# Two-part heads, with scores and transposes by row halves of the array

## The chip, the core and the metric

The kernel runs on one core of a Trainium2 chip. The metric is the device time of one execution in microseconds (us); less is better. The five engines of the core that matter here are TensorE (matrix products and transposes, PE in the rows; its weight loads are PEld), VectorE (DVE), ScalarE (ACT), GpSimd (POOL) and the DMA queues (SP issues most of them). TensorE writes to PSUM, which has eight banks of 512 fp32 values for each of 128 partitions; VectorE and ScalarE read it from there.

## What is computed

Two layers, each followed by `layernorm(x + layer(x))`, on an input of 2 x 4096 x 256 (fp32). The first is a gated linear recurrence over blocks of 512 tokens. The second picks 511 tokens of each of the two batches with a router and runs a transformer block on them. The change lies in its attention, with 16 heads of 16 values:

```
hn = rmsnorm(x_sel, ln1)
q, k = rope(heads(hn @ wq), pos_sel), rope(heads(hn @ wk), pos_sel)
v = heads(hn @ wv)
sc = einsum('bhqd,bhkd->bhqk', q, k) / sqrt(16) + m_sel
a = softmax(sc); o = einsum('bhqk,bhkd->bhqd', a, v) ... @ wo
x2 = x1 + gelu(rmsnorm(x1, ln2) @ w1) @ w2          # x1 = x_sel + o
```

## The kernel before

One program with an order of instructions written out by hand for each engine; engines wait for each other on counting semaphores. The stages follow one another: recurrence (0 to about 173 us), router and choice of tokens, projections and mask for both batches (to 255), attention and FFN of batch 0 (to 366), attention and FFN of batch 1, final normalisation and scatter.

**Precision of the scores.** Products of q and k are made from parts of the numbers. Before, each q and each k is split into three bf16 parts (`parts` on VectorE, nine instructions for a chunk of 128 tokens), laid out in `SLOTS = 6` slots so that one bf16 product over 6 x 16 = 96 rows sums the six wanted products of parts. `turn_split` on TensorE transposes these for each head (32 bf16 transposes a chunk, L970), `copy_turned` brings them from PSUM to `qkT` (q on ScalarE, L1361, k on VectorE, L1805).

**The attention loop.** It runs for each batch over 4 turns `hg` of 4 heads, and in each over 16 units u: 4 chunks c of 128 queries by 4 heads h (`units`). For one unit:

1. `scores` (TensorE, L1006): one product, 128 queries by 512 keys, into one of four banks (`S_BANKS`, a ring of `RING = 4`), six units ahead (`AHEAD`).
2. `masked` (VectorE, L1857): adds the mask, writes SBUF `sm` (a ring of 8) and the row's extreme `nmax`.
3. `below`: subtracts `nmax` in place; even units on VectorE (L1865), odd ones on GpSimd (L672).
4. `turn_scores` (TensorE, L1023): four 128 x 128 fp32 transposes into bank 2 + u % 2; it waits for `below_ready`, and for the exponential of unit u - 2, which used that bank.
5. `exponentials` (ScalarE, L1377): reads the bank, writes `prT` in SBUF.
6. `values` (TensorE, L1045): for the four heads of a chunk together, 16 x 4 products of 32 columns each in four column groups, five units late (`LAG`); banks 4 and 5.

Around it stand `copy_heads`, `copy_pair` (ScalarE), `normalise_heads` (VectorE), `turn_heads` and `turn_pair` (TensorE, L1054 and L1061), once or twice a turn. In the second attention GpSimd also splits `w2` (L628, L631) between its subtractions. All eight banks are in use: 6, 7, 0, 1 for scores, 2 and 3 for turned differences, 4 and 5 for values. While batch 0 is in its FFN, `turn_split` of batch 1 is placed between the second FFN products (L1152).

## Time and profile before

| | |
|---|---|
| median of 3 runs | 479.98 us (479.44 to 481.64) |
| the profiled execution | 479.28 us |
| its span, first to last instruction | 477.5 us |
| mean granted clock of TensorE | 0.993 |
| first attention, first score product to last exponential | 255.1 to 322.4 us |
| second attention | 366.7 to 436.8 us |

The span is what the trace shows of the profiled execution; the 1.8 us between it and that execution's time lie before and behind it. Records of TensorE's products overlap, since it is pipelined: how fast they follow one another is read from their starts. In the rows by stretch the numbers are: the stretch and its length in us, the busy time of PE, PEld, DVE, ACT and POOL with the count of instructions behind each, the granted clock as a share of full speed, the busy share of the DMA engines and GB/s. In the rows by line, `out<-in` are the tiles written and read, with partitions x elements behind them, and `[t <-engine ...]` at the end of a row of a timeline is how long the engine sat idle before it and what released it.

### The profile page before, as it was taken

What the parts mean: (1) busy time and instruction counts of PE and PEld (TensorE: products, weight loads), DVE (VectorE), ACT (ScalarE), POOL (GpSimd) and SP (SyncE); (2) the same over time, 40 slices, a digit from 0 to 9 for tenths busy, and PEclk for the clock granted to TensorE, in tenths of its full rate; (3) what the DMA queues carried; (4) which work ended last, traced back from release to release, by engine and by line L of the source; (5) the groups of instructions that cost most, each with busy time, mean ns of one, the idle gap of its engine ahead of it and who ended that gap; (6) DMA issues with size and microseconds to landing.
All of it is one profiled execution on the core that took longest, in us unless ns stands there. A gap on an engine that the chain in (4) does not pass through costs nothing.

```text
span 477.5 us, 9894 instructions
## 1 busy us (share of the span) xinstructions
PE 438.4 (92%) x3557; PEld 335.4 (70%) x3557; DVE 383.8 (80%) x1173; ACT 241.3 (51%) x431; POOL 294.2 (62%) x295
## 2 busy tenths in 40 slices
PE   8798999999999987999998999997998999998893
PEld 5587888777777743476775777775796777676692
DVE  4878898788998799868989999865966999881773
ACT  3436555565545527024665665655434666564640
POOL 8366667776677742076665998842000999991374
PEclk9999999999999999998999999999999999999998
DMA  7713442234421211046981000000000000000011
GB/s 237 264 45 91 123 140 91 88 92 136 126 89 46 71 62 45 1 129 213 321 263 47 1 3 2 1 3 0 2 1 0 1 4 1 1 2 2 1 40 50
DMA packets 29256, 33.88 MB, mean 71 GB/s; under 512 B 5748, under 2 KB 24856, under 8 KB 29208
## 3 DMA queue, kind: packets, MB, share of 16 engines
q1 hardware_dynamic: 22976, 24.78, 16.0%
q0 software_dynamic: 3520, 8.40, 6.0%
q8 instruction: 29, 0.48, 0.4%
q10 hardware_dynamic: 2712, 0.06, 0.3%
q14 instruction: 19, 0.16, 0.1%
HBM read 19.59 MB, written 13.63 MB: 70 GB/s over the span
## 4 chain that ended last, share of the span: by engine, by line
PE 38%; POOL 16%; DVE 10%; issue 4%; ACT 3%; POOLq 0%; DVEq 0%
POOL arena L672 9%; PE ps L1023 7%; PE ps L1045 4%; PE ps L1006 4%; PE ps L1117 3%; PE ps L1152 3%; PE ps L708 3%; PE ps L970 2%; PE ps L842 2%; POOL arena L519 2%; PE ps L938 2%; PE ps L1123 1%; PE ps L977 1%; POOL w_lo L631 1%; PE ps L1143 1%
## 5 line engine op out<-in xcount | busy, mean ns | idle before, releaser
L672 POOL TENSOR_SCALAR arena<-arena,nmax 128x511 f32<-128x511 f32 x64 | 108.4, 1705 | 46.6 <-DVE nmax L1857 46.3
L1377 ACT ACTIVATE big<-ps 128x512 f32<-128x512 f32 x128 | 76.0, 600 | 57.5 <-PE ps L1023 54.4
L1857 DVE CUSTOM_DVE_ANT_0 arena<-ps,nmask 128x511 f32<-128x511 f32 x128 | 83.6, 681 | 7.8 <-PE ps L1006 5.5
L1023 PE MATMUL ps<-ident,arena 128*128 128x128 f32 x512 | 77.7, 274 | 2.4 <-POOL arena L672 1.6
L1023 PEld LDWEIGHTS ps<-ident,arena 128*128 128x128 f32 x512 | 59.5, 140 | 20.3 <-issue 10.1
L741 PE MATMUL ps<-wgd_hi,x_hi 128*128 128x512 f32 x128 | 51.6, 403 | 0.0
L1006 PE MATMUL ps<-arena 96*128 96x512 bf16 x128 | 48.2, 383 | 3.3 <-DVE nmax L1857 2.1
L743 PE MATMUL ps<-wgd_hi,x_lo 128*128 128x512 f32 x128 | 50.5, 395 | 0.0
L742 PE MATMUL ps<-wgd_lo,x_hi 128*128 128x512 f32 x128 | 50.4, 394 | 0.0
L519 POOL TENSOR_TENSOR arena<-arena 128x512 f32<-128x512 f32 x30 | 38.7, 1291 | 9.6 <-DVE arena L1501 7.9
L533 POOL TENSOR_TENSOR rq<-vq,minus_half 128x4 f32<-128x4 f32 x16 | 16.2, 1010 | 35.3 <-DVE v L1530 35.3
L1262 ACT ACTIVATE ob_sb<-arena,nb,rq 128x256 f32<-128x256 f32 x64 | 33.1, 590 | 8.2 <-POOL nb L537 8.1
L1865 DVE TENSOR_SCALAR arena<-arena,nmax 128x511 f32<-128x511 f32 x64 | 36.8, 575 | 0.0
L528 POOL TENSOR_TENSOR r<-v,minus_half 128x8 f32<-128x8 f32 x16 | 26.7, 1670 | 7.7 <-DVE v L1530 7.7
L1476 DVE TENSOR_TENSOR x_lo<-ps,x_hi 128x512 fp32r<-128x512 f32 x32 | 21.9, 685 | 10.6 <-ACT x_hi L1233 10.6
L708 PE MATMUL ps<-ones_b 128*128 128x512 bf16 x106 | 27.0, 379 | 2.7 <-DVE arena L1496 1.5
L1254 ACT CAST h_parts<-arena 48x512 fp32r<-48x512 f32 x16 | 9.9, 621 | 37.4 <-DVE arena L1489 37.4
L1496 DVE TENSOR_TENSOR arena<-ps,arena 128x512 f32<-128x512 f32 x32 | 21.8, 682 | 8.0 <-PE ps L760 8.0
L743 PEld LDWEIGHTS ps<-wgd_hi,x_lo 128*128 128x128 f32 x128 | 24.0, 188 | 5.7
L741 PEld LDWEIGHTS ps<-wgd_hi,x_hi 128*128 128x128 f32 x128 | 24.1, 188 | 5.0
L742 PEld LDWEIGHTS ps<-wgd_lo,x_hi 128*128 128x128 f32 x128 | 24.1, 188 | 5.0
L1245 ACT ACTIVATE arena<-ps 128x512 f32<-128x512 f32 x32 | 19.1, 598 | 16.3 <-PE ps L753 14.3
(266 smaller groups left out, 1013.0 us busy)
## 6 DMA issues: line engine op xcount, KB each, us to landing
arena<-in_L_attn_x SPq DMA_DIRECT2D x16, 512.0 KB, 4.8
out<-ob_sb SPq DMA_DIRECT2D x16, 512.0 KB, 3.1
w_sb<-in_L_ffn_w SPq DMA_DIRECT2D x2, 1024.0 KB, 10.7
mt_scratch<-nmask SPq DMA_DIRECT2D x8, 256.0 KB, 6.3
mt_scratch<-big SPq DMA_DIRECT2D x8, 256.0 KB
big<-in_L_attn_Wg SPq DMA_DIRECT2D x1, 256.0 KB, 4.2
big<-in_L_attn_WD SPq DMA_DIRECT2D x1, 256.0 KB, 5.1
wqk<-in_L_ffn_wq SPq DMA_DIRECT2D x1, 256.0 KB, 8.3
```

Of the source, the lines that this page charges most:

```text
L519: pool.tensor_tensor(s, s, u_sb[q][:, :, :], ALU.subtract).then_inc(s_ready, 1)
L672: pool.tensor_scalar(sm[n % SM_RING][:, 0:K - 1], sm[n % SM_RING][:, 0:K - 1], nmax[:, c, h:h + 1], None, ALU.subtract).then_inc(below_rea ...
L708: pe.matmul(ps[:, bank, :], ones_b[:, :], ones_wide, start=True, stop=True)
L741: pe.matmul(o, hi, wgd_hi[:, c, :], start=(c == 0), stop=False)
L742: pe.matmul(o, hi, wgd_lo[:, c, :], start=False, stop=False)
L743: pe.matmul(o, lo, wgd_hi[:, c, :], start=False, stop=False)
L1006: pe.matmul(ps[:, bank, :], qkT[0][:, hg * HG + h:hg * HG + h + 1, c * P:(c + 1) * P], qkT[1][:, hg * HG + h:hg * HG + h + 1, :], start=Tr ...
L1023: mm = pe.transpose(ps[:, 2 + u % 2, k * P:(k + 1) * P], sm[n % SM_RING][:, k * P:(k + 1) * P], ident[:, :])
L1262: last = act.activation(ob_sb[G % 2][:, t, :], s_sb[G % 2][:, t, :], ACT.Identity, bias=nb[G % 2][:, t:t + 1], scale=rq[:, b, n.start + t: ...
L1377: act.activation(prT[c % 2][:, h, :, :], ps[:, 2 + u % 2, :].rearrange("p (k n) -> p k n", k=C), ACT.Exp, scale=-1.0).then_inc(prT_ready, 1)
L1857: dve.tensor_tensor_reduce(sm[n % SM_RING][:, 0:K - 1], ps[:, S_BANKS[b][u % RING], 0:K - 1], nmask[b][:, c, 0:K - 1], 1.0, 3.4e38, ALU.ad ...
L1865: dve.tensor_scalar(sm[n % SM_RING][:, 0:K - 1], sm[n % SM_RING][:, 0:K - 1], nmax[:, c, h:h + 1], None, ALU.subtract).then_inc(below_read ...
```

## The change

- A head's q and k are split into two parts, a high one in fp32r and the fp32 rest, in `SLOTS = 4` slots of 16: 64 rows a head, so two heads (2 x 64 rows) share one 128-row transpose. `high` (ScalarE) copies the high parts into two slots, `parts` (VectorE, two subtractions) the rests. `turn_split` makes 16 fp32 transposes a chunk instead of 32 bf16 ones; `qT` and `kT` are fp32r.
- `scores` takes units in pairs: two products over 64 rows each, one in the upper, one in the lower half of the array's rows.
- `turn_scores` takes units in pairs too. The differences of a unit are transposed in halves of 64 rows by 64 x 64 pieces of the identity. `turn_halves` with r = 0 turns the upper half of the first unit (into bank 2) and the lower half of the second (into bank 3) by turns, with r = 1 the other halves. Between the two stand the score products of the pair six units ahead and a wait for `halves_turned`, that is for the first halves to be done.
- `below` is dealt out by `BELOW = "DPADPDPA"`: of eight units three to VectorE, three to GpSimd, two to ScalarE (an activation with scale -1 and `nmax` as bias, three units ahead of the exponential).

```diff
@@ -44,8 +44,7 @@
 SPLIT = 2
 POS = 11
 ABOVE = 14
-SLOTS = 6
-ER = SLOTS * HD
+SLOTS = 4
 HG = 4
 HP = 32
 TURNS = H // HG
@@ -58,6 +57,8 @@
 S_BANKS = ((6, 7, 0, 1), (0, 1, 6, 7))
 M_BANKS = (4, 6, 5, 7)
 LAG = 5
+BELOW = "DPADPDPA"
+A_AHEAD = 3
 PARTS = ((range(C),), ((C - 1,), (0, 1), (2,)))
 ORDER = tuple(tuple(c for part in parts for c in part) for parts in PARTS)
 FB = F // P
...
@@ -394,6 +396,15 @@
         def unit_number(b, hg, u):
             return (hg + b * TURNS) * UNITS + u

+        def below_count(n, who):
+
+            return n // len(BELOW) * BELOW.count(who) + BELOW[:n % len(BELOW) + 1].count(who)
+
+        def below_done(n):
+
+            who = BELOW[n % len(BELOW)]
+            return below_ready["DPA".index(who)], below_count(n, who)
+
         def second_out(b, c):

             return ps[:, S_BANKS[b][c], 0:D] if b == B - 1 else ps[:, 6 + c // 2, (c % 2) * D:(c % 2 + 1) * D]
...
@@ -677,11 +688,12 @@
                 for hg in range(2):
                     values_of(b, hg)
                 for hg in range(TURNS):
-                    for u in range(1, UNITS, 2):
-                        below(b, hg, u)
+                    for u in range(UNITS):
+                        if BELOW[u % len(BELOW)] == "P":
+                            below(b, hg, u)
                         if u == 9 and 0 < hg < TURNS - 1:
                             values_of(b, hg + 1)
-                        if b == B - 1 and hg in (1, 2):
+                        if b == B - 1 and u % 2 and hg in (1, 2):
                             split_w2((hg - 1) * FB + u // 2)
                 for half in range(2):
                     rsqrt(b, half)
...
@@ -957,18 +969,16 @@
                     project_qk(b, c, ps[:, 4 + c % 2, :])
                     project_values(b, c)

-            psb = ps[:, :, :].bitcast(BF16)
-
             def turn_split(b, c):

                 done = c + b * C
-                pe.wait_ge(e_ready, done + 1)
                 for m in ((1, 0) if done == C - 1 else range(2)):
+                    pe.wait_ge(e_ready, 2 * done + (2 if done == C - 1 else 1 + m))
                     for half in range(2):
                         pe.wait_ge((qT_ready, kT_ready)[m], done * 2)
-                        for h in range(8):
-                            mm = pe.transpose(psb[0:ER, 2 * m + half, h * P:(h + 1) * P],
-                                              e_sb[c % 2][:, m, 8 * half + h, :, :], ident_b[:, :])
+                        for g in range(4):
+                            mm = pe.transpose(ps[:, 2 * m + half, g * P:(g + 1) * P],
+                                              e_rows[c % 2][:, m, 4 * half + g, :], ident[:, :])
                         mm.then_inc(eT_done[2 * m + half], 1)

             def project_out(b, c, groups):
...
@@ -986,43 +996,62 @@
                 pe.wait_ge(kT_ready, (b + 1) * C * 2 - 1)

                 def scores(hg, u):
-                    c, h = units[u]
+
+                    for v in (u, u + 1):
+                        c, h = units[v]
+                        n = unit_number(b, hg, v)
+                        bank = S_BANKS[b][v % RING]
+                        if hg_is(hg, 0):
+                            if v < RING and bank < 2:
+                                pe.wait_ge(qT_ready, (b + 1) * C * 2 - 1 + bank)
+                            elif h == 0:
+                                pe.wait_ge(qT_ready, (b * C + c) * 2 + 1)
+                        if not first(b, hg) or v >= RING:
+
+                            pe.wait_ge(sm_ready, n - RING + 1)
+                        if hg_is(hg, 0) and bank >= 6:
+
+                            if b > 0:
+                                pe.wait_ge(x2_ready, (b - 1) * C + C)
+                            else:
+                                pe.wait_ge(nm_ready[0], C)
+                    for v in (u, u + 1):
+                        c, h = units[v]
+                        g, rows = (hg * HG + h) // 2, slice(h % 2 * 64, h % 2 * 64 + 64)
+                        pe.matmul(ps[:, S_BANKS[b][v % RING], :], qT[rows, g, c * P:(c + 1) * P], kT[rows, g, :],
+                                  start=True, stop=True).then_inc(s_done, 1)
+
+                def turn_scores(hg, u):
+
+                    for v in (u, u + 1):
+                        n = unit_number(b, hg, v)
+                        pe.wait_ge(*below_done(n))
+                        if hg_is(hg, 0) and v == 0:
+                            pe.wait_ge(qT_ready, (b + 1) * C * 2)
+                            pe.wait_ge(kT_ready, (b + 1) * C * 2)
+                        if first(b, hg) and v == 0:
+
+                            pe.wait_ge(zeroed, 3)
+                        if not first(b, hg) or v >= 2:
+
+                            pe.wait_ge(prT_ready, n - 1)
+
+                    turn_halves(b, hg, u, 0)
+
+                def turn_halves(b, hg, u, r):
                     n = unit_number(b, hg, u)
-                    bank = S_BANKS[b][u % RING]
-                    if hg_is(hg, 0):
-                        if u < RING and bank < 2:
-                            pe.wait_ge(qT_ready, (b + 1) * C * 2 - 1 + bank)
-                        elif h == 0:
-                            pe.wait_ge(qT_ready, (b * C + c) * 2 + 1)
-                    if not first(b, hg) or u >= RING:
-
-                        pe.wait_ge(sm_ready, n - RING + 1)
-                    if hg_is(hg, 0) and bank >= 6:
-
-                        if b > 0:
-                            pe.wait_ge(x2_ready, (b - 1) * C + C)
-                        else:
-                            pe.wait_ge(nm_ready[0], C)
-                    pe.matmul(ps[:, bank, :], qkT[0][:, hg * HG + h:hg * HG + h + 1, c * P:(c + 1) * P],
-                              qkT[1][:, hg * HG + h:hg * HG + h + 1, :], start=True, stop=True).then_inc(s_done, 1)
-
-                def turn_scores(hg, u):
-
-                    n = unit_number(b, hg, u)
-                    pe.wait_ge(below_ready[u % 2], n // 2 + 1)
-                    if hg_is(hg, 0) and u == 0:
-                        pe.wait_ge(qT_ready, (b + 1) * C * 2)
-                        pe.wait_ge(kT_ready, (b + 1) * C * 2)
-                    if first(b, hg) and u == 0:
-
-                        pe.wait_ge(zeroed, 3)
-                    if not first(b, hg) or u >= 2:
-
-                        pe.wait_ge(prT_ready, n - 1)
+                    if r:
+                        pe.wait_ge(halves_turned, n // 2 + 1)
                     for k in range(C):
-                        mm = pe.transpose(ps[:, 2 + u % 2, k * P:(k + 1) * P],
-                                          sm[n % SM_RING][:, k * P:(k + 1) * P], ident[:, :])
-                    mm.then_inc(belowT_done, 1)
+                        for v in range(2):
+                            at = (r + v) % 2 * 64
+                            mm = pe.transpose(ps[:, 2 + v, k * P + at:k * P + at + 64],
+                                              sm[(n + v) % SM_RING][at:at + 64, k * P:(k + 1) * P],
+                                              ident[at:at + 64, at:at + 64])
+                            if r and k == C - 1:
+                                mm.then_inc(belowT_done, 1)
+                    if r == 0:
+                        mm.then_inc(halves_turned, 1)

                 def values(hg, c):
                     turn = hg + b * TURNS
...
@@ -1079,14 +1108,16 @@

                 def turn_body(hg):
                     if hg_is(hg, 0):
-                        for u in range(AHEAD):
+                        for u in range(0, AHEAD, 2):
                             scores(hg, u)
                     for u in range(UNITS):
-                        if u + AHEAD < UNITS:
-                            scores(hg, u + AHEAD)
-                        elif not hg_is(hg, TURNS - 1):
-                            scores(hg + 1, u + AHEAD - UNITS)
-                        turn_scores(hg, u)
+                        if u % 2 == 0:
+                            turn_scores(hg, u)
+                            if u + AHEAD < UNITS:
+                                scores(hg, u + AHEAD)
+                            elif not hg_is(hg, TURNS - 1):
+                                scores(hg + 1, u + AHEAD - UNITS)
+                            turn_halves(b, hg, u, 1)
                         late(hg, u)
                         if not hg_is(hg, 0):
                             late(hg - 1, u + UNITS)
...
@@ -1358,13 +1389,24 @@
             def copy_turned(b, c):
                 for half in range(2):
                     act.wait_ge(eT_done[half], c + b * C + 1)
-                    act.copy(qkT[0][:, 8 * half:8 * half + 8, c * P:(c + 1) * P],
-                             ps[:, :, :].bitcast(BF16)[0:ER, half, :].rearrange("r (h n) -> r h n", h=8)
-                             ).then_inc(qT_ready, 1)
+                    act.copy(qT[:, 4 * half:4 * half + 4, c * P:(c + 1) * P],
+                             ps[:, half, :].rearrange("r (g n) -> r g n", g=4)).then_inc(qT_ready, 1)
+
+            def high(b, c):
+                done = c + b * C
+                act.wait_ge(rope_ready[b], c + 1)
+                for m, s in enumerate((slice(0, 4, 2), slice(0, 4, 3))):
+                    if done >= 2:
+                        act.wait_ge(eT_done[2 * m], done - 1)
+                        act.wait_ge(eT_done[2 * m + 1], done - 1)
+                    src = qk[b][:, c:c + 1, m * D:(m + 1) * D].rearrange("p o (h k) -> p h o k", h=H)
+                    act.copy(e_sb[c % 2][:, m, :, s, :].bitcast(F32R), src.broadcast_to((P, H, 2, HD))).then_inc(e_parts, 1)

             def split(b):
                 for c in range(C):
                     copy_turned(b, c)
+                    if c < 2:
...
@@ -1375,7 +1417,14 @@

                         act.wait_ge(pv_done, (hg + b * TURNS) * C + c - 1)
                     act.activation(prT[c % 2][:, h, :, :], ps[:, 2 + u % 2, :].rearrange("p (k n) -> p k n", k=C),
-                                   ACT.Exp, scale=-1.0).then_inc(prT_ready, 1)
+                                   ACT.Exp, scale=1.0 if BELOW[u % len(BELOW)] == "A" else -1.0).then_inc(prT_ready, 1)
+
+                def below(hg, u):
+                    c, h = units[u]
+                    n = unit_number(b, hg, u)
+                    act.wait_ge(sm_ready, n + 1)
+                    act.activation(sm[n % SM_RING][:, 0:K - 1], sm[n % SM_RING][:, 0:K - 1], ACT.Identity,
+                                   bias=nmax[:, c, h:h + 1], scale=-1.0).then_inc(below_ready[2], 1)

                 def copy_heads(hg, cs):
                     act.wait_ge(pv_done, (hg + b * TURNS) * C + cs[-1] + 1)
@@ -1392,7 +1441,13 @@

                 def turn_body(hg):
                     for u in range(UNITS):
+                        if BELOW[u % len(BELOW)] == "A" and u < A_AHEAD and hg_is(hg, 0):
+                            below(hg, u)
+                    for u in range(UNITS):
                         exponentials(hg, u)
+                        v = u + A_AHEAD
+                        if BELOW[v % len(BELOW)] == "A" and (v < UNITS or hg < TURNS - 1):
+                            below(hg + v // UNITS, v % UNITS)
                         if u == 2 and not hg_is(hg, 0):
                             copy_heads(hg - 1, range(C))
                         if u == 8 and hg == 2:
...
@@ -1415,6 +1470,8 @@
                     if b == B - 1:
                         act.wait_ge(gelu_ready, b * FB + f + 1)
                         act.copy(hid_hi[:, f, :], hidden_sb[:, f, :]).then_inc(hid_hi_ready, 1)
+                    elif f in (3, 5):
+                        high(b + 1, f // 2 - 1)

             for c in range(2):
                 copy_first_hnT(0, c)
...
@@ -1802,33 +1863,17 @@
             def copy_turned(b, c):
                 for half in range(2):
                     dve.wait_ge(eT_done[2 + half], c + b * C + 1)
-                    dve.tensor_copy(qkT[1][:, 8 * half:8 * half + 8, c * P:(c + 1) * P],
-                                    ps[:, :, :].bitcast(BF16)[0:ER, 2 + half, :].rearrange(
-                                        "r (h n) -> r h n", h=8)).then_inc(kT_ready, 1)
+                    dve.tensor_copy(kT[:, 4 * half:4 * half + 4, c * P:(c + 1) * P],
+                                    ps[:, 2 + half, :].rearrange("r (g n) -> r g n", g=4)).then_inc(kT_ready, 1)

             def parts(b, c):
                 done = c + b * C
                 dve.wait_ge(rope_ready[b], c + 1)
...
+                for m, (hi, lo) in enumerate(((slice(0, 4, 2), slice(1, 4, 2)), (slice(0, 4, 3), slice(1, 3)))):
+                    dve.wait_ge(e_parts, 2 * done + m + 1)
+                    src = qk[b][:, c:c + 1, m * D:(m + 1) * D].rearrange("p o (h k) -> p h o k", h=H)
+                    dve.tensor_tensor(e_sb[c % 2][:, m, :, lo, :], src.broadcast_to((P, H, 2, HD)),
+                                      e_sb[c % 2][:, m, :, hi, :], ALU.subtract).then_inc(e_ready, 1)
...
@@ -1879,7 +1924,7 @@
                 def turn_body(hg):
                     for u in range(UNITS):
                         masked(hg, u)
-                        if u % 2:
+                        if u and BELOW[(u - 1) % len(BELOW)] == "D":
                             below(hg, u - 1)
                         if u == 10 and not hg_is(hg, 0):
                             normalise_heads(hg - 1, range(C))
```

## Rows read from the trace of the kernel before

**Rows 1.** The page: busy time, share of the span and instructions of each engine.

```profile
PE 438.4 (92%) x3557; PEld 335.4 (70%) x3557; DVE 383.8 (80%) x1173; ACT 241.3 (51%) x431; POOL 294.2 (62%) x295
```

**Rows 2.** Busy us of each engine in stretches of the span, and granted clock.

```profile
263.00:318.00 55.00, 54.66 (x741) 42.09 (x738) 49.62 (x148) 34.68 (x61) 50.04 (x31) 1.00 0.01 2
...
376.00:420.00 44.00, 42.40 (x548) 31.69 (x546) 41.50 (x118) 26.72 (x46) 44.00 (x40) 1.00 0.01 2
...
215.00:219.00 4.00, 4.00 (x13) 2.20 (x12) 2.91 (x11) 0.00 (x0) 1.85 (x2) 0.57 0.79 292
```

**Rows 3.** The chain that ended last, in the first attention: start us, us, what.

```profile
262.94 1.01 PE ps L1045 x32
...
266.77 1.01 PE ps L1045 x32
```

**Rows 4.** Timeline of the first attention, TensorE and ScalarE: start us, us, engine, line.

```profile
273.63 0.38 PE L1006 MATMUL ps<-arena 96*128 96x512 bf16 x1
...
273.85 0.60 PE L1023 MATMUL ps<-ident,arena 128*128 128x128 f32 x4
...
274.38 0.81 PEld L1045 LDWEIGHTS ps<-big,arena 128*32 128x32 f32 x32 [0.17 <-issue]
274.38 1.08 PE L1045 MATMUL ps<-big,arena 128*32 128x128 f32 x32
...
277.22 1.10 ACT L1377 ACTIVATE big<-ps 128x512 f32<-128x512 f32 x2
```

**Rows 5.** Groups of instructions by line and form: busy us, mean ns, idle before.

```profile
L672 POOL TENSOR_SCALAR arena<-arena,nmax 128x511 f32<-128x511 f32 x64 | 108.4, 1705 | 46.6 <-DVE nmax L1857 46.3
...
L1023 PE MATMUL ps<-ident,arena 128*128 128x128 f32 x512 | 77.7, 274 | 2.4 <-POOL arena L672 1.6 <-ACT big L1377 0.7
...
L1865 DVE TENSOR_SCALAR arena<-arena,nmax 128x511 f32<-128x511 f32 x64 | 36.8, 575 | 0.0
```

**Rows 6.** Timeline near the end of the first attention: handoffs between TensorE and ScalarE.

```profile
316.13 0.60 ACT L1377 ACTIVATE big<-ps 128x512 f32<-128x512 f32 x1 [1.00 <-PE ps L1023]
...
316.84 0.42 PEld L1023 LDWEIGHTS ps<-ident,arena 128*128 128x128 f32 x4 [0.55 <-issue]
316.87 0.63 PE L1023 MATMUL ps<-ident,arena 128*128 128x128 f32 x4 [0.34 <-ACT big L1377]
316.88 1.26 ACT L1377 ACTIVATE big<-ps 128x512 f32<-128x512 f32 x2
```

**Rows 7.** Timeline of the first microseconds, TensorE: four transposes of 16 rows.

```profile
6.11 0.60 PE L781 MATMUL ps<-ident,nmask 16*128 16x16 f32 x4
```

**Rows 8.** ScalarE: a row of its timeline, one of the groups by line.

```profile
104.29 2.07 ACT L1262 ACTIVATE ob_sb<-arena,nb,rq 128x256 f32<-128x256 f32 x4
...
L1417 ACT CAST hid_hi<-big 128x512 fp32r<-128x512 f32 x8 | 5.0, 621 | 0.3
```

**Rows 9.** Timeline: first scores and last exponential of both attentions, one GpSimd start.

```profile
255.11 1.03 PE L1006 MATMUL ps<-arena 96*128 96x512 bf16 x4
...
321.79 0.60 ACT L1377 ACTIVATE big<-ps 128x512 f32<-128x512 f32 x1 [0.49 <-PE ps L1023]
...
366.68 0.60 PE L1006 MATMUL ps<-arena 96*128 96x512 bf16 x2
...
368.95 10.31 POOL L672 TENSOR_SCALAR arena<-arena,nmax 128x511 f32<-128x511 f32 x6 [37.68 <-DVE nmax L1857]
...
436.15 0.60 ACT L1377 ACTIVATE big<-ps 128x512 f32<-128x512 f32 x1 [0.49 <-PE ps L1023]
```

**Rows 10.** Timeline of the split: last chunk of batch 0, then of batch 1.

```profile
251.54 1.96 PE L970 MATMUL ps<-ident_b,arena 128*96 128x128 bf16 x32 [0.43 <-DVE arena L1805]
...
359.31 1.92 ACT L1361 COPY arena<-ps 96x1024 bf16<-96x1024 bf16 x2 [3.38 <-PE ps L970]
...
361.37 1.96 PE L970 MATMUL ps<-ident_b,arena 128*96 128x128 bf16 x32 [0.76 <-ACT arena L1361]
```

**Rows 11.** Timeline of TensorE just before its slow stretch.

```profile
211.94 3.90 PE L842 MATMUL ps<-arena 128*128 128x60 bf16 x32
```

More of the change, by code:

```diff
@@ L145, in build @@
         hid_hi, hid_lo = under(("hid_hi", [P, FB, K], F32R), ("hid_lo", [P, FB, K], F32R))
+        qT, kT = under(*[(n, [P, H // 2, K], F32R) for n in ("qT", "kT")])
         arena = sb("arena", [P, (XBUF + 4) * T * D])
@@ L248, in build @@
         rope_a, rope_b = (arena2[:, n * 1024:(n + 1) * 1024].rearrange("p (c n) -> p c n", c=2) for n in range(2))
[L249 to L250 removed]
+        e_rows = [arena2[:, 4096 + e * 2048:6144 + e * 2048].rearrange("p (m g r) -> p m g r", m=2, g=H // 2)
+                  for e in range(2)]
+        e_sb = [arena2[:, 4096 + e * 2048:6144 + e * 2048].rearrange(
             "p (m h s k) -> p m h s k", m=2, h=H, s=SLOTS) for e in range(2)]
[L252 to L253 removed]
         at_hi = arena2[:, 0:B * P * NT // 2].bitcast(BF16).rearrange("p (b h n) -> p b h n", b=B, h=P)
@@ L324, in build @@
         sm_ready = sem("sm_ready")
-        below_ready = sems("below_ready")
+        below_ready = sems("below_ready", 3)
         belowT_done = sem("belowT_done")
+        halves_turned = sem("halves_turned")
         prT_ready = sem("prT_ready")
@@ L1367, in split @@
                     copy_turned(b, c)
+                    if c < 2:
+                        high(b, c + 2)
             def attention(b):
@@ L1427, in _ @@
                 value(0, c - 1)
+            high(0, 0)
             copy_qk(0, C - 1)
             value(0, C - 1)
+            high(0, 1)
             copy_mask_rows(0, range(3))
@@ L1443, in _ @@
             copy_turned(0, 0)
+            high(0, 2)
             copy_qk(1, 2)
@@ L1446, in _ @@
             copy_turned(0, 1)
+            high(0, 3)
             value(1, 3)
@@ L1946, in _ @@
                     angles(1)
+                elif c == 2:
                     parts(0, 0)
```

35 lines of the change are left out of this document (6 added, 29 removed).

## The prediction, made before the changed kernel was run

> **What bounds the kernel now.** I read the page first: TensorE is busy 92% of the span [rows 1]. Such a share mixes stages, so the next view is the busy time by stage [rows 2]. In the steady part of the first attention (263 to 318 us) TensorE works 54.66 of 55 us; in that of the second (376 to 420 us) GpSimd works all 44. ScalarE has time left in both (34.68 of 55 us, 26.72 of 44).
>
> The chain of waits says the same of the first attention: it runs through TensorE, one group of values (L1045) every 3.83 us, so 0.96 us a unit [rows 3]. The timeline shows what fills that: score product, transposes and a quarter of the values take 0.22, some 0.46 and 0.27 us (products from 273.63 on, transposes from 273.85, 1.08 for the values of four units) [rows 4]. In the second attention it is 32 subtractions of 1.7 us on GpSimd [rows 5], with the weight split between them.
>
> What the reader should look at for this change is the pair of PSUM banks between the transposes (TensorE) and the exponentials (ScalarE). Before, unit u uses bank 2 + u % 2: while ScalarE reads one bank, TensorE fills the other. That is why a unit can cost 0.96 us although its transposes take 0.63 from first start to last end and its exponential another 0.60 behind them [rows 6].
>
> **The change: a ring.** A pair of units now writes half of each unit's transposes into both banks, waits, and then writes the other halves. `turn_scores` therefore waits, ahead of the first half, for both exponentials of the pair before (for the pair's second unit, `prT_ready` at n - 1 is the exponential of unit u - 1). And the exponentials of either unit wait for `belowT_done`, which only the last step of the second half raises. Transposes of a pair, its two exponentials, transposes of the next pair: these no longer overlap. Queued behind the waiting transposes stand the next scores, six units ahead, so nobody waits for them. The price is the length of this ring, from the end of one pair's last exponential to that of the next:
>
> - End of an exponential to the first weight load: 0.11 us (316.13 + 0.60 to 316.84); 0.03 more to the first transpose [rows 6].
> - First half: 8 transposes of 64 rows, four steps of two row halves. Fewer rows do not shorten a transpose: four with 16 rows and a 16-wide identity took 0.60 us [rows 7], four of 128 by 128 take 0.60 to 0.63 [rows 4, 6]; less the 0.27 us of the last one [rows 5] either follow one another at 0.11 us. So a step costs 0.11 us if the two halves of the array load and multiply at the same time, and 0.22 if one weight load follows the other. No row of this trace shows two row halves. The nearest, four column groups in L1045, do multiply side by side (32 in 1.08 us) but load weights one after the other (32 in 0.81 us) [rows 4]. Those share the array's rows, these do not, so I take 0.11 and keep 0.22 as a rival. Three steps of 0.11 and 0.27 for the last: 0.60.
> - The wait for `halves_turned`: a handoff of 0.11 like the one above, and 0.03. The two score products stand in it. The last step of the first half starts 0.47 us into the ring and the second half could start at 0.88; a score product needs 0.22 of TensorE [rows 4], so two side by side cost nothing. If they run one after the other, the second half starts at 0.47 + 0.11 + 0.44 = 1.02, 0.14 late: the upper bound.
> - Second half: 0.60. Handoff to ScalarE: 0.04 (316.87 + 0.63, and the second exponential's start, 316.88 + 1.26 - 0.60) [rows 6].
> - Two exponentials back to back: 1.10 (277.22) [rows 4].
>
> Sum: 0.11 + 0.03 + 0.60 + 0.14 + 0.60 + 0.04 + 1.10 = 2.62 us for two units, where two cost 1.92. The values (1.08 for two pairs) run while ScalarE holds the banks and cost nothing.
>
> The Trainium skill (TensorEngine Tiling, Key Properties) says that different tiles can load weights and multiply in parallel; no row here shows it for row halves. By that sentence the ring is 2.62 us, by serial loads 3.50. The same page of the Trainium skill (Restrictions and Gotchas, Gotcha 1) speaks against the change: row tiles cannot use one PSUM bank at once, so row tiling takes more banks; all eight are taken here.
>
> **Onto the ring come** things that ScalarE does between a pair's two exponentials. `BELOW` hands ScalarE two subtractions in eight units. That of unit 7 is issued behind exponential 4, inside a pair: 8 in an attention. The trace has no such operation; near it are 0.62 us for 512 elements in SBUF and 2.07 us for four activations of 256 elements with two column operands [rows 8]. I take 0.65, bounds 0.5 and 0.8: 5.2 us an attention. The other one stands between pairs, under the transposes. The copies of heads and pairs behind units 2, 8 and 10 are inside pairs as well: four of 512 elements at 0.50 (1.10 - 0.60, as for a second exponential) and a shorter one, 2.2 us.
>
> **An attention** is then 32 x 2.62 + 5.2 + 2.2 = 91.2 us behind its start. The first pair needs a subtraction of GpSimd, as odd units do now. In the second attention that starts at 368.95, 2.27 us behind the first scores; with 1.72 for it and 0.11, the ring starts after 4.1 us [rows 5, 9], and I take the same for the first. That makes 95.3 us each. Now they take 67.3 (255.11 to 321.79 + 0.60) and 70.1 (366.68 to 436.15 + 0.60) [rows 9]. Loss: 28.0 + 25.2 = 53.2 us. What follows the last exponential is unchanged.
>
> Taking subtractions off VectorE and GpSimd (64 each before, 48 each after, 32 on ScalarE) gains nothing, since in 2.62 us a pair neither is late: GpSimd's three in eight units are 5.2 of 10.5 us, even with the weight split, and VectorE's work was 49.62 us for some 57 units [rows 2], 1.74 a pair.
>
> **The split of heads.** VectorE's nine instructions a chunk become two, with two copies of `high` on ScalarE. ScalarE's two copies of turned heads, 1.92 us together [rows 10], become two of 512 elements, 1.10 like the exponentials [rows 4]. TensorE's 32 bf16 transposes took 1.96 us [rows 10]; 16 in fp32 take 15 x 0.11 + 0.27 = 1.92: nothing. Between the attentions the second FFN product covers all this but for the last chunk, which waits for ScalarE's copies (359.31 to 361.23, transposes at 361.37): 0.8 us gained. Ahead of the first attention TensorE waited 0.43 us for VectorE's copy before the last chunk [rows 10]: 0.4 gained at most there. `high` stands on ScalarE ahead of projections, mask rows and gelus, 1.24 us for a chunk [rows 8]; ScalarE's idle time covers it; without that cover, one chunk's worth ahead of each attention is 2.5 us. I take -1.2, bounds -4 and +2.5.
>
> **Sum.** The profiled execution took 479.28 us (its span 477.5, 1.8 around it), 0.7 below the median 479.98. 479.28 + 53.2 - 1.2 = 531.3; I say 531. Its own bounds: a handoff of 0.04 at `halves_turned` (-0.07 for 64 pairs, -4.5), the subtraction at 0.5 (-2.4), the split (-2.8); up: serial scores (+9), the subtraction at 0.8 (+2.4), the split (+3.7). 521 to 546.
>
> **The rivals.**
> - *The weight loads of the row halves follow each other.* Eight steps cost 0.11 more: 0.88 us a pair, 64 pairs, 56 us: 587. For it: the loads of L1045 [rows 4]. Against: those share the array's rows.
> - *TensorE's clock falls.* Its mean was 0.57 at 215 to 219 us, so mostly the lower of its two levels (1.2 of 2.4 GHz), behind 3.9 us in which TensorE had run 60-column products without a gap [rows 2, 11]. In the new ring it would be idle or in 64-column transposes most of the time. At half clock the eight steps cost 0.88 more a pair and the values, 2.16 us, no longer fit under 1.10, 0.5 more: 64 x 1.4 = 90 us, 621; clock falling now and then, anything from 535 on. Against: 1.00 throughout both attentions [rows 2].
> - *Faster.* Were the ring shorter than the other engines' pace, VectorE would bind: 49.62 less an eighth of 57 units at 0.575 us is 45.5 us for 57 units [rows 2, 5], 0.80 each; 64 of them instead of 0.96 are 10 us less in the first attention, 13 in the second, 455 us. It decides where the ring falls under 1.9 - 0.2 us a pair, so if sixteen transposes and their wait took 0.4 us instead of 1.3. Rows 7 speak against it, and the exponentials alone are 1.10.
>
> The Trainium skill (TensorE: Matmul & The Clock Gate, Part 4: PE-mode transpose) says that transposes do not count as busy for the clock in the same way; here the clock stays at 1.00 with transposes filling half of TensorE's time [rows 2]. By that rule the second rival is likelier than I make it.
>
> **How the numbers follow.** Ring of 2.6 us: 0.57, the forecast. Serial loads 0.25. Clock 0.11. Faster 0.05. No difference 0.02. A measurement of this kernel tells about 0.5% (2.4 us) from no change, and the first three cases are far beyond it: slower 0.93, same 0.02, faster 0.05. The first two hold 0.82 and give the range, 519 to 592; the likeliest alone has 521 to 546.
>
> **What would show it.** Right: in both attentions ScalarE idles about 1.5 us before the first exponential of each pair, waiting for the second half of the transposes; the first half waits for the second exponential; pairs follow at 2.6 us, each half takes 0.6; TensorE is busy two thirds of the time. Serial loads: halves of 1.0 us, pairs at 3.5. Clock: granted row below 1.00 in the attentions. Wrong altogether: an exponential of one pair beside transposes of the next, or pairs under 1.9 us apart.

## Result and profile after

The changed kernel takes 526.25 us (median of four runs, 524.99 to 527.43) against 479.78 us (479.44 to 481.64): 1.0959 times as long, 95% interval 1.0919 to 1.1. The profiled execution took 526.98 us, 47.7 more than that of before.

Where do the 47.7 us lie? In the timeline, an attention runs from its first score product to the end of its last exponentials (in the changed kernel L1021 and L1419, transposes L1048, values L1074):

```profile
254.63 0.73 PE L1021 MATMUL ps<-kT,qT 64*128 64x512 f32 x4
...
346.80 1.08 ACT L1419 ACTIVATE big<-ps 128x512 f32<-128x512 f32 x2 [2.90 <-PE ps L1048]
...
391.38 0.50 PE L1021 MATMUL ps<-kT,qT 64*128 64x512 f32 x2
...
483.35 1.08 ACT L1419 ACTIVATE big<-ps 128x512 f32<-128x512 f32 x2 [2.89 <-PE ps L1048]
```

That is 93.25 and 93.05 us, where before had 67.28 and 70.07 [rows 9]: 25.97 + 22.98 = 48.95 lost. The rest of the kernel gained the other 1.25: 0.48 ahead of the first attention, 0.79 between the two (391.38 - 347.88 against 366.68 - 322.39).

The timeline of three pairs of units in the first attention, TensorE at full clock (an engine's wait stands in brackets):

```profile
280.10 0.43 PE L1048 MATMUL ps<-ident,arena 64*128 64x64 f32 x7
...
280.35 0.47 PE L1021 MATMUL ps<-kT,qT 64*128 64x512 f32 x1
...
280.39 0.48 PE L1021 MATMUL ps<-kT,qT 64*128 64x512 f32 x1
...
282.35 0.36 PEld L1048 LDWEIGHTS ps<-ident,arena 64*128 64x128 f32 x8 [1.38 <-DVE arena L1910]
282.38 0.47 PE L1048 MATMUL ps<-ident,arena 64*128 64x64 f32 x8 [1.27 <-ACT big L1419]
...
282.94 0.45 PE L1048 MATMUL ps<-ident,arena 64*128 64x64 f32 x8
...
283.42 1.09 ACT L1419 ACTIVATE big<-ps 128x512 f32<-128x512 f32 x2 [0.57 <-PE ps L1048]
...
284.65 0.46 PE L1048 MATMUL ps<-ident,arena 64*128 64x64 f32 x8 [0.25 <-ACT big L1419]
```

The ring is there: first half at 282.38, second half at 282.94, both exponentials from 283.42 to 284.51, next first half at 284.65. No exponential of one pair runs beside transposes of the next. A turn takes 2.27 us. Eight half transposes take 0.47 from the first start to the last end, with their eight loads (0.36) beside them, and the two score products start 0.04 apart (280.35, 280.39).

The waits by engine say how often (total us, times, longest):

```profile
ACT big L1419 <- PE ps L1048: 85.3, 64, 2.9
DVE arena L1902 <- PE ps L1021: 57.4, 56, 2.2
PE ps L1048 <- ACT big L1419: 50.3, 48, 1.8
```

All 64 pairs make ScalarE wait for the transposes. ScalarE had waited for TensorE before the change as well (1.00 and 0.49 in [rows 6, 9]); what is new is the other direction: before, the transposes waited 0.7 us in all for ScalarE [rows 5], now 50.3. Now the same steps 15 us earlier, and the busy time by stretches (PE, PEld, DVE, ACT, POOL, then the granted clock):

```profile
267.29 0.69 PE L1048 MATMUL ps<-ident,arena 64*128 64x64 f32 x8
...
270.21 0.69 PE L1048 MATMUL ps<-ident,arena 64*128 64x64 f32 x8 [1.27 <-ACT big L1419]
...
271.79 1.93 PE L1074 MATMUL ps<-big,arena 128*32 128x128 f32 x32
273.66 0.59 PE L1048 MATMUL ps<-ident,arena 64*128 64x64 f32 x6
```

```profile
258.00:348.00 90.00, 64.04 (x1082) 50.46 (x1086) 53.27 (x155) 46.55 (x86) 41.24 (x26) 0.81 0.01 2
392.00:485.00 93.00, 65.11 (x1102) 50.99 (x1106) 54.24 (x161) 48.36 (x87) 50.83 (x42) 0.83 0.01 2
254.60:259.40 4.80, 2.08 (x25) 1.27 (x24) 4.14 (x13) 1.86 (x4) 2.27 (x2) 1.00 0.00 0
265.00:275.00 10.00, 8.72 (x126) 7.00 (x123) 4.71 (x14) 4.48 (x8) 3.85 (x3) 0.50 0.01 2
285.00:305.00 20.00, 12.81 (x282) 10.23 (x278) 13.52 (x40) 11.61 (x21) 10.98 (x8) 1.00 0.01 2
```

From 265 to 275 the granted clock is 0.50, the lower level, 1.2 GHz; before, it was 1.00 in the steady part of both attentions [rows 2]. The fall comes behind the first 4.8 us of the attention, in which TensorE was busy for 2.08 us. A turn of the ring is then 2.92 us, or 3.45 where the values (1.93 us) stand in it. So two theories have to be told apart: the ring, and the clock.

### The profile page after: what moved, and what is told of

Its sections match the earlier page's. It is cut to its first block, busy times and chain, and to the rows that moved or that the text cites. A ratio compares the mean times of both kernels' runs of the same rounds, so it can differ in the third digit from the quotient of the medians.

```text
span 525.2 us, 10691 instructions
## 1 busy us (share of the span) xinstructions
PE 436.9 (83%) x3941; PEld 337.9 (64%) x3941; DVE 360.7 (69%) x1101; ACT 256.8 (49%) x479; POOL 268.7 (51%) x279
## 4 chain that ended last, share of the span: by engine, by line
PE 45%; ACT 11%; issue 7%; POOL 6%; DVE 5%; POOLq 0%; ACTq 0%; DVEq 0%
PE ps L1048 11%; ACT big L1419 7%; PE ps L1074 5%; PE ps L1021 4%; PE ps L1148 3%; PE ps L950 3%; PE ps L980 3%; PE ps L1183 3%; PE ps L720 2%; PE ps L854 2%; POOL arena L530 2%; PE ps L987 2%; PE ps L955 1%; PE ps L1154 1%; PE ps L1083 1%
## 5 line engine op out<-in xcount | busy, mean ns | idle before, releaser
L683 POOL TENSOR_SCALAR arena<-arena,nmax 128x511 f32<-128x511 f32 x48 | 83.7, 1745 | 113.0 <-DVE nmax L1902 112.8
L1902 DVE CUSTOM_DVE_ANT_0 arena<-ps,nmask 128x511 f32<-128x511 f32 x128 | 85.6, 686 | 58.7 <-PE ps L1021 57.4
L1419 ACT ACTIVATE big<-ps 128x512 f32<-128x512 f32 x128 | 72.3, 596 | 85.3 <-PE ps L1048 85.3
L1048 PE MATMUL ps<-ident,arena 64*128 64x64 f32 x1024 | 65.5, 252 | 53.4 <-ACT big L1419 50.3
L1048 PEld LDWEIGHTS ps<-ident,arena 64*128 64x128 f32 x1024 | 52.5, 158 | 72.8 <-issue 48.1
L1021 PE MATMUL ps<-kT,qT 64*128 64x512 f32 x128 | 37.1, 554 | 2.7 <-DVE nmax L1902 2.2
L1426 ACT ACTIVATE arena<-arena,nmax 128x511 f32<-128x511 f32 x32 | 22.9, 717 | 8.8 <-DVE nmax L1902 8.8
```

The costliest lines, as they stand in the source:

```text
L683: pool.tensor_scalar(sm[n % SM_RING][:, 0:K - 1], sm[n % SM_RING][:, 0:K - 1], nmax[:, c, h:h + 1], None, ALU.subtract).then_inc(below_rea ...
L1021: pe.matmul(ps[:, S_BANKS[b][v % RING], :], qT[rows, g, c * P:(c + 1) * P], kT[rows, g, :], start=True, stop=True).then_inc(s_done, 1)
L1048: mm = pe.transpose(ps[:, 2 + v, k * P + at:k * P + at + 64], sm[(n + v) % SM_RING][at:at + 64, k * P:(k + 1) * P], ident[at:at + 64, at:a ...
L1419: act.activation(prT[c % 2][:, h, :, :], ps[:, 2 + u % 2, :].rearrange("p (k n) -> p k n", k=C), ACT.Exp, scale=1.0 if BELOW[u % len(BELOW ...
L1902: dve.tensor_tensor_reduce(sm[n % SM_RING][:, 0:K - 1], ps[:, S_BANKS[b][u % RING], 0:K - 1], nmask[b][:, c, 0:K - 1], 1.0, 3.4e38, ALU.ad ...
```

## Experiments

Each kernel is compared with the kernel before (medians 480.1 to 480.6 us) on the same chip.

**Transposes by unit again.** All else of the change stays.

```diff
...
-for k in range(C):
-    for v in range(2):
-        at = (r + v) % 2 * 64
-        mm = pe.transpose(ps[:, 2 + v, k * P + at:k * P + at + 64],
-                          sm[(n + v) % SM_RING][at:at + 64, k * P:(k + 1) * P], ident[at:at + 64, at:at + 64])
+for k in range(C):
+    mm = pe.transpose(ps[:, 2 + u % 2, k * P:(k + 1) * P],
+                      sm[n % SM_RING][:, k * P:(k + 1) * P], ident[:, :])
...
```

> The changed kernel with one part undone: the differences are transposed unit by unit again, four 128 x 128 transposes into bank 2 + u % 2, each waiting for the exponential two units back. Heads in two parts, scores by row halves and the dealing of the subtractions stay. Ring theory (the loss is the loss of overlap on the two banks): TensorE needs 0.12 + 0.46 + 0.27 = 0.85 us a unit, VectorE 0.80, so about 60 us for each attention instead of 93, and 463 us in all, below the kernel before. Rival (two-part heads, scores by row halves, or ScalarE's subtractions cost the time): above 500 us, most of the loss stays.

Measured: 482.79 us, ratio 1.0044 (1.0021 to 1.0066). 43 of the 46 us go with the transposes in halves, as expected; this run takes away the crossing of two units over two banks and the halves themselves at once (the run with row halves without the shared banks, below, takes away the crossing alone). But the gain expected on top is missing. The timeline of TensorE shows why (values, products of a pair, eight transposes; the last two lines are of the kernel before):

```profile
280.97 1.08 PE L1059 MATMUL ps<-big,v_odd 128*32 128x128 f32 x32
281.99 0.49 PE L1020 MATMUL ps<-kT,qT 64*128 64x512 f32 x2
282.41 1.10 PE L1037 MATMUL ps<-ident,arena 128*128 128x128 f32 x8
283.44 0.49 PE L1020 MATMUL ps<-kT,qT 64*128 64x512 f32 x2
283.87 1.10 PE L1037 MATMUL ps<-ident,arena 128*128 128x128 f32 x8
284.90 1.08 PE L1059 MATMUL ps<-big,v_odd 128*32 128x128 f32 x32
...
271.78 0.60 PE L1023 MATMUL ps<-ident,arena 128*128 128x128 f32 x4
272.22 0.38 PE L1006 MATMUL ps<-arena 96*128 96x512 bf16 x1
```

Four units take 3.93 us without a gap, where before took 3.83 [rows 3]. A pair of products takes 0.42 although both run side by side, no better than two by 0.22 [rows 4], and eight transposes take 1.03 to the next products, where two fours of before take 2 x 0.44 (271.78 to 272.22).

**Half the exponentials' columns.** The exponentials read 256 of 512 columns; half of the attention weights are left out.

```diff
-act.activation(prT[c % 2][:, h, :, :], ps[:, 2 + u % 2, :]...
+act.activation(prT[c % 2][:, h, 0:2, :], ps[:, 2 + u % 2, 0:256]...
```

> The changed kernel, but each exponential reads and writes 256 of its 512 columns (half of the attention weights are left out, so the output is not the reference's). Ring theory: an exponential is some 0.22 us shorter, two stand on the ring of each pair, 64 pairs: 28 us less, 498 us, perhaps a little below as TensorE idles less. Rival (TensorE's own work or its clock sets the pace): ScalarE has half of its time idle, so no change, 526 us.

Measured: 490.17 us, ratio 1.0207 (1.0182 to 1.0231): 36 us less than the change. ScalarE is busy for 49% of the changed kernel's span, and yet what it works less comes off the time: its work stands on the path. Two exponentials take 0.66 us here instead of 1.09, which is 28 us for 64 pairs; the rest of the 36 comes together with a higher clock, 0.97 in this stretch where the change has 0.82:

```profile
286.27 0.66 ACT L1419 ACTIVATE big<-ps 128x256 f32<-128x256 f32 x2 [0.57 <-PE ps L1048]
...
264.00:318.00 54.00, 41.43 (x892) 33.32 (x890) 41.88 (x124) 26.35 (x67) 33.38 (x21) 0.97 0.01 3
```

**No subtractions on ScalarE.** `BELOW = "DPDPDPDP"` in place of `"DPADPDPA"`, with the ring kept.

> The changed kernel with the subtractions dealt out as before, to VectorE and GpSimd by turns, none on ScalarE. Ring theory: the eight of ScalarE's in an attention that stand between the two exponentials of a pair go, some 0.6 us each: 16 x 0.6 = 10 us less, 516 us. Rival (VectorE or GpSimd would be late without ScalarE's share): no gain or a loss, 526 us or more.

Measured: 519.53 us, ratio 1.0769 (1.0696 to 1.0841): 7 us less by the medians, 9 by the ratios ((1.0959 - 1.0769) x 479.8). ScalarE's subtractions stand on the ring, somewhat cheaper than the 10.4 us of the prediction.

**The row halves not alternating.** Four transposes in one row half, then four in the other, instead of in turn.

```diff
-for k in range(C):
-    for v in range(2):
+for v in range(2):
+    for k in range(C):
```

> The changed kernel with the eight transposes of a half in another order: four of the first unit's row half, then four of the second's, instead of by turns. If a half takes only 0.46 us because neighbours in different row halves run side by side, then four in the same row half follow one another at 0.06 us instead of 0.03: 0.24 more for each half, 64 pairs: 31 us more, 557 us. Rival (each 64-row transpose costs 0.03 us in any order): 526 us.

Measured: 525.36 us, ratio 1.096 (1.0915 to 1.1005): no difference, and a half still takes 0.47:

```profile
280.43 0.47 PE L1048 MATMUL ps<-ident,arena 64*128 64x64 f32 x8 [1.20 <-ACT big L1419]
...
281.03 0.47 PE L1048 MATMUL ps<-ident,arena 64*128 64x64 f32 x8
```

The order makes no difference, but that does not settle whether the two row halves work at the same time: the expectation took it that four transposes written one behind the other also start one behind the other. The trace says otherwise. In this run two transposes of the second half have started by 281.04. In the run with row halves without the shared banks (below), four of one row half stand alone: of those at 291.62 only one has started by 291.72, and the four take 0.46, as long as eight in both halves. The rows are one of this run and two of that one; the numbers in brackets count transposes, then loads, that had started:

```profile
281.00:281.04 0.04, 0.01 (x2) 0.04 (x3) 1.00 0.00 0
...
291.60:291.72 0.12, 0.10 (x1) 0.11 (x2) 1.00 0.00 0
...
291.62 0.46 PE L1042 MATMUL ps<-ident,arena 64*128 64x64 f32 x4
```

So transposes of one row half follow one another at 0.06 us (0.11 behind the first), and the two halves run beside each other whichever order they are written in. The transposes of a half also share a bank in both runs; whether row half or bank sets the 0.06 no run tells apart.

**Work for TensorE's idle time.** Eight more score products, with a result that nobody reads, behind every second pair.

```diff
+elif u % 4 == 3 and (hg < TURNS - 1 or u + 8 < UNITS):
+    pe.wait_ge(sm_ready, unit_number(b, hg, u) + 5)
+    for i in range(8):
+        rows = slice(i % 2 * 64, i % 2 * 64 + 64)
+        pe.matmul(ps[:, S_BANKS[b][(u + 3 + i % 2) % RING], :], qT[rows, 0, 0:P], kT[rows, 0, :], ...
```

> The changed kernel with eight score products more behind every second pair (those after which no values are due), into score banks that are free then and whose contents nobody reads, so that TensorE idles less. Clock theory (part of the loss is TensorE's clock, 0.81 and 0.83 in the mean of the two attentions): the clock stands at 1.00, a pair takes 2.27 us throughout instead of 2.8, some 9 us less in each attention, 508 us. Rival (the extra products delay the next pair, or the clock does not matter to a ring that waits mostly for ScalarE): 526 us or more.

Measured: 514.23 us, ratio 1.0701 (1.0655 to 1.0747): added work makes the kernel 12 us faster. The granted clock went up with it (0.81 and 0.88 in the same stretches of the change):

```profile
258.00:330.00 72.00, 58.76 (x1034) 45.20 (x1036) 48.74 (x146) 39.90 (x72) 39.06 (x24) 0.95 0.01 3
...
376.00:420.00 44.00, 36.13 (x474) 28.66 (x472) 28.70 (x79) 20.61 (x37) 19.82 (x17) 0.92 0.01 1
```

**Row halves without the shared banks.** Each unit keeps its own bank, turns its upper half and then its lower half, and the lower half of one stands beside the upper half of the next.

```diff
+rows = slice(64 * f, 64 * f + 64)
+for k in range(C):
+    mm = pe.transpose(ps[:, 2 + u % 2, k * P + 64 * f:k * P + 64 * f + 64],
+                      sm[n % SM_RING][rows, k * P:(k + 1) * P], ident[rows, rows])
+mm.then_inc(belowT_done if f else halves_turned, 1)
...
+turn_half(hg, u, 1)
+turn_half(hg, u + 1, 0)
```

> The changed kernel with its row halves kept but the ring cut: each unit again has a bank of its own for both halves of its transposes, first its upper half, then, when that is done, its lower half; the lower half of a unit and the upper half of the next stand side by side, and a unit waits only for the exponential two units back. Ring theory: ScalarE's exponential of one unit runs beside the transposes of the next again, some 1.9 us a pair, 465 to 485 us. Rival (the row halves themselves, or the waits between them, cost the time): above 510 us.

Measured: 502.89 us, ratio 1.0485 (1.043 to 1.0539): half of the loss remains, more than expected. TensorE's loads and transposes of a pair:

```profile
291.02 0.40 PEld L1042 LDWEIGHTS ps<-ident,arena 64*128 64x128 f32 x8
291.02 1.06 PE L1042 MATMUL ps<-ident,arena 64*128 64x64 f32 x12
...
291.61 0.33 PEld L1042 LDWEIGHTS ps<-ident,arena 64*128 64x128 f32 x4 [0.20 <-PE ps L1042]
...
292.23 0.26 PEld L1042 LDWEIGHTS ps<-ident,arena 64*128 64x128 f32 x3 [0.28 <-issue]
292.26 0.30 PE L1042 MATMUL ps<-ident,arena 64*128 64x64 f32 x2 [0.18 <-ACT big L1412]
```

Two waits a pair are left: 0.20 for the other half of the same bank, and about 0.28 for the exponential two units back. The view of waits counts 12.1 us of the one and 15.2 us of the other, 60 times each. And in the first 20 us of either attention the clock was 0.83 and 0.59 in place of 1.00. So cutting the crossing alone gives 23 us back, and a unit in two halves still has a handoff that a unit in one piece doesn't have.

**Before, with score products over 64 rows.** To see what row tiling costs by itself: two of the six parts of the product are left out (64 of 96 rows), all else is the kernel before.

```diff
-pe.matmul(ps[:, bank, :], qkT[0][:, ...], qkT[1][:, ...], start=True, stop=True)
+pe.matmul(ps[:, bank, :], qkT[0][0:64, ...], qkT[1][0:64, ...], start=True, stop=True)
```

> The kernel before with its score products over 64 of the 96 rows (two of the six products of parts are left out of the scores). Asked because the run with transposes by unit, whose only row halves are the scores, took 0.42 us from a pair of score products to the transposes behind them, no less than two products of before. Theory (TensorE must empty before it goes from products over all rows to one over a row half, and back): 0.18 + 0.11 us more for each unit, 0.29 x 64 in the first attention, somewhat less in the second, about 510 us. Rival (a product over 64 rows costs what one over 96 does): 480 us.

Measured: 500.48 us, ratio 1.0456 (1.0379 to 1.0534): less work, 20 us more. The same steps as in [rows 4]:

```profile
283.11 0.39 PE L1006 MATMUL ps<-arena 64*128 64x512 bf16 x1
283.42 0.66 PE L1023 MATMUL ps<-ident,arena 128*128 128x128 f32 x4
284.01 0.39 PE L1006 MATMUL ps<-arena 64*128 64x512 bf16 x1
```

Product to transposes 0.31 instead of 0.22, transposes to the next product 0.59 instead of 0.44: 0.24 us for going to the row half and back. The Trainium skill (TensorEngine Tiling, Key Properties) says that a change of the tiling mode drains TensorE; the trace agrees in so far as both ways take longer, by 0.09 and 0.15, but no row shows the drain itself.

**By unit, with products over all 128 rows.** A score is then the sum of two heads' (this part is changed), and TensorE stays untiled between products and transposes.

```diff
-g, rows = (hg * HG + h) // 2, slice(h % 2 * 64, h % 2 * 64 + 64)
+g, rows = (hg * HG + h) // 2, slice(0, P)
...
```

> The kernel with the transposes by unit (e1), but each score product contracts all 128 rows instead of one head's 64, so a score is the sum of two heads' (that part of the computation is changed). If TensorE pays for going from row halves to all rows and back, then both payments go: products of a pair to the next transposes 0.44 us (two by 0.22) where e1 has 0.42, eight transposes to the next products 0.88 where e1 has 1.03, values 0.51 as before: 1.83 a pair instead of 1.96. 64 pairs by 0.13 are 8 us: 475, bounds 473 to 479, since VectorE and GpSimd are not far behind. Rival: the switch is free and the 1.03 has another cause, so that two products one after the other are only added work: 64 by 0.2 more, 492 or so; nothing changes: 483.

Measured: 483.37 us, ratio 1.0068 (1.0044 to 1.0093), no gain.

```profile
282.31 0.73 PE L1020 MATMUL ps<-kT,qT 128*128 128x512 f32 x2
282.88 1.04 PE L1037 MATMUL ps<-ident,arena 128*128 128x128 f32 x8
283.67 0.71 PE L1020 MATMUL ps<-kT,qT 128*128 128x512 f32 x2
284.26 1.12 PE L1037 MATMUL ps<-ident,arena 128*128 128x128 f32 x8
285.31 1.08 PE L1059 MATMUL ps<-big,v_odd 128*32 128x128 f32 x32
```

Half of the expectation holds. Eight transposes take 0.79 to an untiled product (282.88 to 283.67) and 1.03 to a row-half one, 0.24 more; ahead of the values, whose groups of 32 columns are tiles too, it is 1.05 (284.26 to 285.31). Not all of the 0.24 need be the way into the tiles: at the 0.11 of [rows 4] eight transposes take 0.88, from which 1.03 is 0.15 away, as in the run before, and 0.79 is 0.09 less than that, which no run explains. But the way back costs nearly nothing here: behind the start of the last product of a pair, transposes follow after 0.34 (0.58 less the 0.24 between the two, 0.73 - 0.49) here and after some 0.39 in the kernel by unit (0.42 less 0.03). What I had taken for a drain behind these products is mostly that an fp32r product holds the transposes behind it longer than the bf16 product of before, 0.22 [rows 4]. And a pair of untiled products takes 0.57 to 0.59 to its transposes, where the row halves took 0.42, which takes back what is saved behind the transposes.

**By unit, products of two pairs together,** so that there are half as many changes.

```diff
-if u % 2 == 0:
-    scores(hg, u + AHEAD)
+if u % 4 == 0:
+    for v in (u + AHEAD, u + AHEAD + 2):
...
+            scores(hg, v)
...
```

> The kernel with the transposes by unit (e1), with the score products of two pairs issued together every four units, so half as many changes between row halves and all rows. If the changes cost, four units now take 2 x (0.42 + 1.03) + 1.02 = 3.92 us; then 0.42 + 0.22 for four products, 16 x 0.11 + 0.15 for the transposes, 1.02 for the values: 3.57. 32 groups by 0.35 are 11 us, less about 1.5 at each attention's start for the longer run of products: 474, bounds 470 to 480. Rival: the four products need four empty banks at once and VectorE, busy for 49.7 of 60 us, empties them late, so that TensorE waits in front of each group: 484 or more, with TensorE idle in the steady part.

Measured: 482.83 us, ratio 1.0045 (1.0022 to 1.0068): no gain, by the rival's mechanism (it had 484 or more).

```profile
280.15 0.73 PE L1020 MATMUL ps<-kT,qT 64*128 64x512 f32 x4
...
284.31 0.50 PE L1020 MATMUL ps<-kT,qT 64*128 64x512 f32 x2
285.03 0.50 PE L1020 MATMUL ps<-kT,qT 64*128 64x512 f32 x2 [0.22 <-DVE nmax L1887]
```

Four products take 0.66 to the next transposes (280.15 to 280.81) instead of twice 0.42, but other groups are torn apart, because VectorE has not emptied the banks: 1.16 from 284.31 to the transposes at 285.47.

**Before, with the change's dealing of the subtractions** (`BELOW = "DPADPDPA"`, 48 on VectorE, 48 on GpSimd, 32 on ScalarE, in the kernel before).

```diff
+for u in range(UNITS):
+    exponentials(hg, u)
+    v = u + A_AHEAD
+    if BELOW[v % len(BELOW)] == "A" and (v < UNITS or hg < TURNS - 1):
+        below(hg + v // UNITS, v % UNITS)
...
```

> The kernel before with one part of the change alone: the subtractions dealt to VectorE, GpSimd and ScalarE as DPADPDPA. The first attention is bound by TensorE at 0.96 us a unit and stays; in the second GpSimd's 32 subtractions and the weight split no longer bind: some 3 us less, 477 us. Rival (ScalarE's subtraction stands between an exponential and the next transposes): 480 us or more.

Measured: 479.06 us, ratio 0.9974 (0.995 to 0.9998): the fastest version seen, by a quarter of a per cent, which is less than can be told with confidence from no change. The second attention, which GpSimd bound [rows 2], is 1.5 us shorter here (367.36 to 435.89, 68.5 us).

## Why the prediction was right, and where two of its terms were off

- **The ring** was right as a mechanism, and is shown: by the transposes' waits for ScalarE (50.3 us, before 0.7), by half-width exponentials (36 us less) and by cutting the crossing of the two banks alone (23 us less) or with the halves (43 us less).
- **The length of a turn** was mis-sized: 2.27 us instead of 2.62. The step that failed is "a step costs 0.11 us if the two halves of the array load and multiply at the same time". The two halves did run at the same time; what was wrong is the price, from "Fewer rows do not shorten a transpose", read from transposes of 128 and of 16 rows [rows 4, 7]. Here eight take 0.46, a step of two 0.06, and four of one row half alone follow one another at 0.06 as well. Why those of 16 rows took 0.11 stays open. From the first half's start to the second's it was 0.56 (forecast 0.60 + 0.14), from there to the exponential 0.48 (0.60 + 0.04), the exponentials 1.09 (1.10), and back to the transposes 0.14 (0.14). The transposes make up 0.28 of the 0.35, the handoff between the halves (0.09 instead of 0.14) 0.05. 32 x 0.35 are 11.2 us an attention too much.
- **The two score products beside each other** fit, as forecast.
- **The clock** was given as another case (0.11), with a forecast at 1.00 throughout. It came in part, on top of the ring: with the measured turn an attention is 32 x 2.27 + 5.2 + 2.2 + 4.1 = 84.1 us (the last three as forecast), and 93.2 were measured, 9.1 more. The rows agree: a mean clock of 0.81 over 90 us is 0.38 of it, 34 us, at 0.50; turns there take 3.19 on average (2.92 and 3.45) against 2.27, so 34 x (1 - 2.27 / 3.19) = 9.9 us. Added work that raised the clock gave 12 us of the two attentions' 18 back. At the lower level the rival had a turn 0.88 longer by its transposes and 0.5 by the values; they were 0.65 (2.92 - 2.27) and 0.53 (3.45 - 2.92). That TensorE would idle was rightly named; that the clock must decide between cases was wrong, and it should have been a term of the sum.
- So 531 against 526 is closer than the terms were, by luck: -11.2 and +9.1 an attention nearly cancel (93.2 measured, 95.3 forecast).
- **Serial loads** did not come. The Trainium skill (TensorEngine Tiling, Key Properties) says that tiles load and multiply in parallel; the traces agree for row halves: eight loads in both halves take 0.34 to 0.36 us and four in one 0.33, and eight transposes take 0.47 and four 0.46.
- **Subtractions on ScalarE:** 0.72 us each, of which 0.61 on the ring (forecast 0.65: at 278.27 and 279.37 the exponentials of a pair start 1.10 apart instead of 0.49), 7 to 9 us of the kernel (10.4).
- **The split and the rest:** -1.25 (forecast -1.2), 0.48 ahead of the first attention (0.4) and 0.79 between them (0.8). TensorE's waits of 0.43 and 0.76 before the last chunks [rows 10] are gone.
- **The rival "faster"** asked for a ring under 1.7 us a pair, and the ring took 2.27, so it was not met. The runs add that without any ring the gain would not have come either: a pair of row-half products and the transposes behind it take 1.45 us with the transposes by unit (0.42 + 1.03), where before took 1.32 (2 x 0.22 + 2 x 0.44).

## What to carry to other kernels

When a step is split so that two units share both halves of a double buffer, draw the ring of waits first: the two buffers are then one, and the turn is the sum of both engines' times, however quick each is. Two smaller pieces need not be cheaper where TensorE changes between tiled and untiled products around them, so count these changes and price them from a row. And take the price of a piece from a row of its own size, since a bigger and a smaller one agreed here and both misled. Where a change makes TensorE wait, put the fallen clock in the sum as a term, not only among the rivals.

## What was not expected of the hardware

- 64 x 64 fp32 transposes of one row half follow one another at 0.06 us, 128 x 128 ones at 0.11 [rows 4]; two row halves run beside each other, whether their transposes are written by turns or four and four (four in one half 0.46, eight in both 0.46 to 0.47).
- Eight untiled transposes take 0.79 us to an untiled product and 1.03 to 1.05 to row-half products or column-group values. With bf16 products over 64 rows the way in and back cost 0.15 + 0.09, and less work made the kernel 20 us longer.
- An fp32r score product holds the transposes behind it for 0.34 to 0.39 us from its start, a bf16 one of the same 512 columns for 0.22.
- Eight more products per two pairs, work for nobody, made the kernel 12 us faster, with the granted clock up from 0.81 to 0.95 in the first attention.
